# Layer 0 of a four-layer cross-attention kernel: each engine's order of stages written out by hand with other lags, and one MLP product moved from VectorE to GpSimd

## The reference

```
x1 = x  + SelfAttention(LN1(x))  Wao + bao      softmax(q k^T / 4 * mask - 10000 (1 - mask)) v
x2 = x1 + CrossAttention(LN2(x1), ctx) Wco + bco
y  = x2 + gelu(LN3(x2) W1 + b1) W2 + b2         W1: 256 x 1024, W2: 1024 x 256
gelu(h) = 0.5 h (1 + tanh(0.7978845608 h (1 + 0.044715 h^2)))
```

## Time and profile before

| | |
|---|---|
| median of 3 runs (lowest, highest) | 1527.47 us (1522.78, 1533.39) |
| the profiled execution | 1539.91 us |
| its span, first to last instruction | 1536.9 us |
| layer 0 in it, to the last write of `xs` (L765) | 0 to 647 us |
| layers 1 to 3 | 647 to 1537 us |
| busy over the span: PE, DVE, ACT, POOL | 1308.2, 943.9, 846.2, 491.9 us |
| mean granted PE clock | 0.927 |

### The profile page before, as it was taken

One profiled execution on the slowest core, in us unless ns is written; L12 is line 12 of the kernel. 1 busy time (PEld: TensorE's weight loads), 2 busy tenths in 40 slices (PEclk: granted clock), 3 DMA queues, 4 the chain that ended last, 5 costly groups with the idle time before them and its releaser, 6 DMA issues. The chain is left out here.

```text
span 1536.9 us, 31339 instructions
## 1 busy us (share of the span) xinstructions
PE 1308.2 (85%) x10866; PEld 1042.4 (68%) x10866; DVE 943.9 (61%) x1843; ACT 846.2 (55%) x2494; POOL 491.9 (32%) x490
## 2 busy tenths in 40 slices
PE   5777777777777775589999999999999999997797
PEld 3555566665666554478888887878878788885464
DVE  4566656565656544376667666676666666664354
ACT  4566565556565634365655555555555665653443
POOL 3343333333434321023333333333333333333000
PEclk8889898989888987889999999999999999998899
DMA  4030000000000000010000000000000000000110
GB/s 156 8 142 8 11 7 10 7 10 7 10 7 3 11 1 1 28 42 2 8 1 9 2 1 10 1 9 1 1 10 1 10 1 1 2 1 1 50 41 27
DMA packets 18578, 25.50 MB, mean 17 GB/s; under 512 B 1360, under 2 KB 16912, under 8 KB 18064
## 3 DMA queue, kind: packets, MB, share of 16 engines
q1 hardware_dynamic: 18448, 23.77, 4.7%
HBM read 21.67 MB, written 2.10 MB: 15 GB/s over the span
## 5 line engine op out<-in xcount | busy, mean ns | idle before, releaser
L1017 POOL TENSOR_TENSOR prob<-prob,l_z_inv 128x512 f32<-128x512 f32 x256 | 261.0, 1041 | 469.1 <-DVE l_z_inv L1258 469.1
L1177 ACT ACTIVATE prob<-psum,l_neg_max 128x256 f32<-128x256 f32 x512 | 236.0, 473 | 245.7 <-DVE l_neg_max L1252 245.7
L674 ACT ACTIVATE ring_e<-ring_e,neg_max 128x128 f32<-128x128 f32 x512 | 163.8, 394 | 142.9 <-DVE neg_max L795 142.9
L1252 DVE TENSOR_REDUCE l_neg_max<-psum 128x2 f32<-128x512 f32 x256 | 164.1, 683 | 14.9 <-PE psum L1071 14.9
L568 PE MATMUL psum<-ident,ring_e 128*128 128x128 f32 x512 | 89.7, 304 | 79.7 <-ACT ring_t L681 75.7
L1083 PEld LDWEIGHTS psum<-ident,prob 128*128 128x128 f32 x1024 | 110.8, 142 | 51.6 <-issue 48.0
L1099 PE MATMUL psum<-pT,vs 128*64 128x256 f32 x1024 | 139.9, 394 | 5.5 <-DVE aTl L1268 5.4
L1083 PE MATMUL psum<-ident,prob 128*128 128x128 f32 x1024 | 141.8, 281 | 1.3 <-issue 1.2
L568 PEld LDWEIGHTS psum<-ident,ring_e 128*128 128x128 f32 x512 | 68.3, 157 | 103.1 <-ACT ring_e L674 91.3
L450 POOL TENSOR_TENSOR ring_e<-ring_e,cross_add 128x512 f32<-128x512 f32 x64 | 81.5, 1287 | 169.7 <-DVE ring_e L790 169.7
L1263 DVE COPY pT<-psum 128x512 f32<-128x512 f32 x128 | 88.2, 689 | 57.1 <-PE psum L1083 57.0
(11 more groups left out here) (197 smaller groups left out, 3292.6 us busy)
## 6 DMA issues: line engine op xcount, KB each, us to landing
wz_raw<-wz_in SPq DMA_DIRECT2D x2, 1536.0 KB, 9.1
x_in<-x SPq DMA_DIRECT2D x8, 256.0 KB, 2.7
cT<-ctxT SPq DMA_DIRECT2D x8, 256.0 KB, 2.7
w<-w_in SPq DMA_DIRECT2D x2, 1024.0 KB, 11.5
l_ub<-ctx_in SPq DMA_DIRECT2D x8, 256.0 KB, 3.7
cg<-ctx_in SPq DMA_DIRECT2D x4, 512.0 KB, 3.8
out<-fin SPq DMA_DIRECT2D x4, 512.0 KB, 2.8
wi_raw<-wi_in SPq DMA_DIRECT2D x1, 1536.0 KB, 14.4
```

The source lines that it names most:

```text
L674: last = nc.scalar.activation(e, e, ACT.Exp, bias=neg_max[:, n % RE, h:h + 1])
L1017: pool.tensor_tensor(e, e, z_inv[:, t % RE, h, :].unsqueeze(2).broadcast_to([P, 2, D]), ALU.mult)\
L1177: last = nc.scalar.activation(prob[:, t % RE, h, qt * D:(qt + 1) * D], score_bank[h][:, qt * D:(qt + 1) * D], ACT.Exp, bias=neg_max[:, t % ...
L1252: nc.vector.tensor_reduce(neg_max[:, t % RE, h, :], score_bank[h].rearrange("p (t c) -> p t c", t=2), AX.X, ALU.max, negate=True).then_inc ...
```

## The change

All arithmetic of layer 0 stays, and layers 1 to 3 are untouched. Five things change.

1. **The order.** The loop over 16 steps is replaced on every engine by a written list of calls, `units(stage, s)` (this stage of unit s, counted from the body's first) and `pairs(stage, off)` (this stage of pair g + off). Blank lines part it into 16 slots. The table has them all; "mul" is `multiply`, "max" `maxima`, "exp" `exponentials`, "copy" `copy_turned`, "pv" is `sums` and `times_v`, "inv" is `invert` (the reciprocal, now a stage of its own), "arg" is the new `argument`, "st" `statistics`.

| slot | PE | ACT | DVE | POOL |
|---|---|---|---|---|
| 0 | cv, T0, turn -3 | tanh3, copy -4, exp -2 | mul 0, read cv, max -1, gated3 | add 0 |
| 1 | pv -8, turn -2, q | copy -3, read T0, exp -1 | mul 1, inv -8, max 0 | std2, add 1 |
| 2 | turn -1 | copy -2, exp 0 | mul 2, norm2, mul 3, divide -8, max 1 | add 2 |
| 3 | y0, scores 4, turn 0, T2 | copy -1, read q, exp 1 | max 2, out y0 | add 3 |
| 4 | k, turn 1 | copy 0, read T2, exp 2 | mul 4, max 3 | add 4 |
| 5 | pv -4, turn 2 | copy 1, exp 3, read k | mul 5, inv -4, max 4 | add 5 |
| 6 | y1, turn 3 | copy 2, exp 4 | mul 6, mul 7, divide -4, max 5 | add 6 |
| 7 | f0, scores 8, o, turn 4 | copy 3, exp 5 | out y1, max 6 | add 7 |
| 8 | f1, turn 5 | hidden0, copy 4, exp 6 | mul 8, max 7 | arg0, bias0, add 8 |
| 9 | pv 0, turn 6 | copy 5, hidden1, exp 7 | mul 9, poly0, read o and st1, inv 0, max 8 | add 9 |
| 10 | ck, f2, turn 7 | tanh0, copy 6, exp 8, read ck | mul 10, mul 11, poly1, divide 0, gated0, max 9, norm1 | std1, add 10 |
| 11 | f3, scores 12, turn 8 | hidden2, copy 7, tanh1, exp 9 | poly2, st0, max 10 | arg1, add 11 |
| 12 | T1, turn 9 | copy 8, hidden3, exp 10 | gated1, cross addend, mul 12, max 11 | bias2, std0, add 12 |
| 13 | pv 4, v, turn 10 | read T1, copy 9, exp 11 | mul 13, inv 4, max 12, read v | add 13 |
| 14 | cq, turn 11 | tanh2, copy 10, read cq, exp 12 | mul 14, mul 15, divide 4, poly3, max 13, gated2, norm0 | arg2, add 14, arg3 |
| 15 | co, scores 16, turn 12 | copy 11, exp 13 | read co and st2, max 14 | bias1, add 15 |

2. **The lags.** `exponentials` goes from s - 1 to s - 2, `turn` from s - 2 to s - 3, `copy_turned` from s - 2 to s - 4, the batch product from 6 steps to 9, `divide` from 7 to 10. Self units belong to pair g - 1 (before g), cross units to g - 3 (g - 2), the MLP's first product to g - 4 (g - 3), its second to g - 5 (g - 3). There are 13 bodies; 5 to 7 are the loop.
3. **The product with h** (L749 before, DVE) is `argument` on POOL.
4. **`times_v` is split**: `sums` comes first with a semaphore of its own.
5. **SP**: the three loads for layer 1 come before `next_x(1)`.

```diff
-        BODIES = R0 + 3
+        BODIES = R0 + 5
...
-        LIKE = 5
-        FILLED = [n for s in range(STEPS) for n in BESIDE.get(s, [])]
+        LIKE = 6
+
+        FILLED = [("cv", -3), ("T0", -1), ("q", -1), ("y0", -5), ("T2", -4), ("k", -1), ("y1", -5), ("f0", -4),
+                  ("o", -2), ("f1", -4), ("ck", -2), ("f2", -4), ("f3", -4), ("T1", -2), ("v", -1), ("cq", -2),
+                  ("co", -3)]
...
             a = int(s < U)
-            i = pair(j, g, -2 if a else 0)
+            i = pair(j, g, -3 if a else -1)
...
+            def units(stage, s):
+                if unit(j, g, s):
+                    stage(*unit(j, g, s))
+
+            def pairs(stage, off, *more):
+                if pair(j, g, off) is not None:
+                    stage(pair(j, g, off), g + off, *more)
...
-            next_x(1)
-            next_x(2)
-            next_ctx(1)
-
             for w, src, c in ((wz0_raw, "wz_in", 0), (wz1_raw, "wz_in", 1), (wi0_raw, "wi_in", 0)):
                 sp.dma_start(w[:, :], v[src][c * P:(c + 1) * P, :]).then_inc(l1_weights_in, 16)
...
+            for g in range(1, R0 + 2):
+                if g >= 3:
+                    next_ctx(g - 2)
+                    next_mask(g - 2)
+                if g < R0:
+                    next_x(g)
...
+            def argument(i, p, f):
+                t, h = ring_g[:, f % RH, :], ring_h[:, f % RH, :]
+                pool.wait_ge(*h_poly.at(i, f))
+                nc.gpsimd.tensor_tensor(t, t, h, ALU.mult).then_inc(h_arg.sem, 1)
...
+            def sums(a, i, u, ri, n):
+                pe.wait_ge(ones_made, 2)
+                pe.wait_ge(*probsT_done.at(ri, n + QUAD - 1))
+                pe.wait_ge(*heads_out.at(ri, n // QUAD - 1))
...
             def polynomial(i, f):
...
                 nc.vector.tensor_scalar(t, t, 0.044715, 1.0, ALU.mult, ALU.add).then_inc(h_poly.sem, 1)
-                dve.wait_ge(*h_poly.at(i, f))
-                nc.vector.tensor_tensor(t, t, h, ALU.mult).then_inc(h_arg.sem, 1)
...
+                pairs(linear, -4, "f3")
+                units(scores, 12)
+                units(turn, 8)
+
+                pairs(linear, -2, "T1")
+                units(turn, 9)
+
+                units(sums, 4)
+                units(times_v, 4)
+                pairs(linear, -1, "v")
+                units(turn, 10)
```

More of the change, by code:

```diff
@@ L297, in bodies @@
         def bodies(eng, body):
-            for g in range(3):
+            for g in range(5):
                 body(g, g)
-            with eng.Fori(3, R0) as j:
+            with eng.Fori(5, R0) as j:
                 body(j, LIKE)
@@ L452, in body @@
             def body(j, g):
[L453 to L472, removed]
+                units, pairs = stages(j, g)
+                units(add_mask, 0)
+                pairs(inverse_std, -4, 2)
+                units(add_mask, 1)
+                units(add_mask, 2)
+                units(add_mask, 3)
+                units(add_mask, 4)
+                units(add_mask, 5)
+                units(add_mask, 6)
+                units(add_mask, 7)
+                pairs(argument, -4, 0)
+                pairs(add_bias, -1, 0, x_ao, x_in, "bao", "o")
+                units(add_mask, 8)
+                units(add_mask, 9)
+                pairs(inverse_std, -2, 1)
+                units(add_mask, 10)
+                pairs(argument, -4, 1)
+                units(add_mask, 11)
+                pairs(add_bias, -4, 2, x_mlp, x_2, "b2", "y1")
+                pairs(inverse_std, 0, 0)
+                units(add_mask, 12)
+                units(add_mask, 13)
+                pairs(argument, -4, 2)
+                units(add_mask, 14)
+                pairs(argument, -4, 3)
+                pairs(add_bias, -2, 1, x_co, x_1, "bco", "co")
+                units(add_mask, 15)
             bodies(pool, body)
@@ L583, in times_v @@
                             at, h = (2 * j + t) * PAIR_ROWS, 2 * half + t
[L584 to L592, removed]
+                            last = nc.tensor.matmul(pv_bank[j * PAIR_ROWS:(j + 1) * PAIR_ROWS, half * P:(half + 1) * P],
+                                                    vm[a][:, b, half, at:at + PAIR_ROWS],
+                                                    ring_t[:, (n + j) % RE, h * P:(h + 1) * P], start=t == 0, stop=t == 1)
@@ L593, in times_v @@
                 last.then_inc(pv_done.sem, 1)
             def body(j, g):
[L596 to L617, removed]
@@ new lines, in body @@
+                units, pairs = stages(j, g)
+                pairs(linear, -3, "cv")
+                pairs(linear, -1, "T0")
+                units(turn, -3)
+                units(sums, -8)
+                units(times_v, -8)
+                units(turn, -2)
+                pairs(linear, -1, "q")
+                units(turn, -1)
+                pairs(linear, -5, "y0")
+                units(scores, 4)
+                units(turn, 0)
+                pairs(linear, -4, "T2")
+                pairs(linear, -1, "k")
@@ new lines, in body @@
+                units(turn, 1)
+                units(sums, -4)
+                units(times_v, -4)
+                units(turn, 2)
+                pairs(linear, -5, "y1")
+                units(turn, 3)
+                pairs(linear, -4, "f0")
+                units(scores, 8)
+                pairs(linear, -2, "o")
+                units(turn, 4)
+                pairs(linear, -4, "f1")
+                units(turn, 5)
+                units(sums, 0)
+                units(times_v, 0)
+                units(turn, 6)
@@ L619, in _ @@
+                pairs(linear, -3, "co")
+                units(scores, 16)
+                units(turn, 12)
             pe.wait_ge(consts_made, 1)
@@ new lines, in body @@
+                pairs(tanh, -5, 3)
+                units(copy_turned, -4)
+                units(exponentials, -2)
+                units(copy_turned, -3)
+                pairs(read, -1, "T0")
+                units(exponentials, -1)
+                units(copy_turned, -2)
+                units(exponentials, 0)
+                units(copy_turned, -1)
+                pairs(read, -1, "q")
+                units(exponentials, 1)
+                units(copy_turned, 0)
+                pairs(read, -4, "T2")
@@ new lines, in body @@
+                units(exponentials, 2)
+                units(copy_turned, 1)
+                units(exponentials, 3)
+                pairs(read, -1, "k")
+                units(copy_turned, 2)
+                units(exponentials, 4)
+                units(copy_turned, 3)
+                units(exponentials, 5)
+                pairs(hidden, -4, 0)
+                units(copy_turned, 4)
+                units(exponentials, 6)
+                units(copy_turned, 5)
+                pairs(hidden, -4, 1)
@@ new lines, in body @@
+                units(exponentials, 7)
+                pairs(tanh, -4, 0)
+                units(copy_turned, 6)
+                units(exponentials, 8)
+                pairs(read, -2, "ck")
+                pairs(hidden, -4, 2)
+                units(copy_turned, 7)
+                pairs(tanh, -4, 1)
+                units(exponentials, 9)
+                units(copy_turned, 8)
+                pairs(hidden, -4, 3)
+                units(exponentials, 10)
+                pairs(read, -2, "T1")
@@ L697, in _ @@
+                units(copy_turned, 9)
+                units(exponentials, 11)
+                pairs(tanh, -4, 2)
+                units(copy_turned, 10)
+                pairs(read, -2, "cq")
+                units(exponentials, 12)
+                units(copy_turned, 11)
+                units(exponentials, 13)
             act.wait_ge(w_cols, 16)
```

282 lines of the change are left out of this document (159 added, 123 removed).

## The result

The changed kernel takes **1399.07 us** (1396.74 to 1400.05), the kernel before, on the same chip, 1530.43: a ratio of 0.914 (0.909 to 0.919). The forecast was 1388, its range 1355 to 1460. The profiled execution took 1398.57 with a span of 1396.8, 140.1 less than before; as that execution of before lay 0.6% over its median, 131 of them are the change's.

What follows compares the result with a forecast made beforehand. The prediction held that the order of the queues, not a full engine, bounds layer 0. Its bodies summed to 508 us against 647, and the 139 us less, taken off the median 1527.47, gave 1388, range 1355 to 1460.

Steps and rivals of the forecast that it cites:

- The body: Full body of layer 0: the new order cuts it from 75.1 to 55 us, PE needing 48.1 at high clock.
- the walk: Slot-by-slot pass through the new order with durations from the trace: 51 us a full body, three PE waits remaining.
- The clock: PE in full bodies: runs at the high clock, since no remaining wait is as long as 2.89 us.
- The product on POOL: Product with h: takes 2.8 us a body from DVE, costs POOL 5.1 at 1.28 each, hidden.
- The collisions: DVE's normalise pairs beside POOL additions: up to 2.8 us a body, some already counted; bound below nothing.
- rival B: DVE held by whole POOL instructions: a body of about 62 us, total 1436; chance 0.22 including the ground up to the forecast.
- The start: First bodies of layer 0: x of pair 1 lands at about 36 us, 8 us lost once, bounds 0 and 11.
- The ends: Layer 0's filling and emptying bodies, summed one by one, tail 36 us; with full bodies layer 0 comes to 508.
- Layers 1 to 3: The later layers, 890 us, were taken as untouched, with no change in time.
- C: Full bodies take exactly 51 us and the ends are 12 us shorter: total 1360; chance 0.12.
- D: The chain across four engines stays the bound, PE's clock falls again: body 72 to 75, total 1505 to 1535; chance 0.08.
- E: Only fixed costs move (late x, end, longer lag), the body keeps 75.1 us: total 1546, slower; chance 0.06.

Runs made afterwards that it cites:

- e4: The changed kernel with four slots instead of two for the MLP's tiles (RH = 4): 1384.7 us, ratio 0.903.
- e9: The kernel before with 128 already met waits added on PE between layer 0 and layer 1: 1519.4 us in one execution.
- e1: The changed kernel with the product with h back on DVE, behind the polynomial: 1401.42 us, ratio 0.9155.
- e5: The changed kernel with DVE's constants() moved behind the first normalise of pair 0: 1397.58 us, ratio 0.910.
- e6: The changed kernel with constants() behind pair 0's first normalise and x of pair 1 issued ahead of the three 1536 KB loads: 1394.21 us, ratio 0.908.

## Why the prediction was right, and where its terms were off

**The body (55; measured 54.5).** The mechanism held: the order was the bound, and PE is now. The 48.1 us of PE's need were too few: at full clock e4 shows 50.3, and the 4 us added to the walk covered that. Three PE waits were named, 2.6 us. Two are there, 2.3 us, at turns 8 and 9 instead of 9 and 12, both behind ACT's `hidden` 2. The walk had it wait for nothing; it waits 2.19 us for a slot of `ring_h`, and with four slots both waits are gone. DVE's wait ahead of the reciprocal, 2 us in the walk, is 7.4 in the body.

**The clock.** I took the high level; 0.97 was measured in the full body, 1.00 in e4, against 0.86 of the earlier trace rows. The tail, where PE stands again, is at 0.83. The clock accounts for a third of the gain, the 7.0 of 20.6 us above; a body of before still took 72.6 us at 0.92 (e9).

**The product on POOL.** Priced 1.28 us, measured 1.27. The Trainium skill (GPSIMD Engine Reference, section 4.1) has GpSimd about twice as slow with two inputs, from which the prediction estimated 2.4 us a body lost. The factor agrees (1.27 against 0.69), and still e1 shows a gain of 1.9 us in the full body: POOL is busy for only 32.5 of 54.5 us. The tail is 4.4 us shorter in e1, where the sum had 2.4 for POOL's part.

**The collisions (within the 4 us allowed).** Lines of the full body, busy us, mean ns, idle before:

```profile
L885 DVE SCALAR_TENSOR_TENSOR hid<-ring_g,ring_h 128x512 f32<-128x512 f32 x5 | 5.3, 1060 | 0.0
...
L442 POOL TENSOR_TENSOR ring_g<-ring_g,ring_h 128x512 f32<-128x512 f32 x4 | 5.1, 1270 | 4.7 <-DVE ring_g L878 4.7
...
L846 DVE TENSOR_SCALAR ln<-x,mean_var,rstd 128x256 f32<-128x256 f32 x4 | 3.7, 971 | 0.0
```

`normalise` took a mean of 640 ns in the body before, now 971, `gated` 863, now 1060. With the product back on DVE (e1) they take 642 and 849 again, so the move is the cause. That is 4 x 0.33 + 5 x 0.20 = 2.3 us in this window, where the earlier trace rows gave up to 2.8. One of rival B's signs thus showed, longer `normalise` and `gated`, without its price: DVE comes to 44.7, not to 58.

**The start (8 us lost to x of pair 1; measured 3.1).** x landed near the 36 forecast: DVE went on at 34.6. The step that failed is the first multiply at 20.5, taken from the earlier trace rows: I missed that `constants()` now stands ahead of pair 0's `normalise`. Two delays lay one over the other. e5 takes away the first and the second grows to 9.38 us; e6 takes away both.

**The ends.** The term mis-sized is the sum's last: layer 0 ended at 519.4 instead of 508. By boundaries (forecast, its bodies cut at slot 12 by the lengths of the slots, and measured): start 72.5, 68.7; body 2 to 3 41, 47.4; 3 to 4 48.5, 50.9; four full ones 219, 217.0; the next 46, 46.7; from there to the last cross product's sum 45, 47.0; the tail 36, 41.9. The tail was taken as 33.8 plus POOL's part. But y0 of pair 6, which ran ahead of the last cross product's sum before (the first line below), now comes behind it, so that both second products of pairs 6 and 7 stand in the tail. The last wait for `gated` is 7.49 us instead of 4.24.

```profile
607.43 3.72 PE L510 MATMUL psum<-w,hid 128*128 128x256 f32 x16
```

```profile
480.00 5.41 PE L536 MATMUL psum<-w,hid 128*128 128x256 f32 x16 [2.54 <-DVE hid L885]
...
506.29 2.64 DVE L885 SCALAR_TENSOR_TENSOR hid<-ring_g,ring_h 128x512 f32<-128x512 f32 x2
508.98 9.93 PE L536 MATMUL psum<-w,hid 128*128 128x256 f32 x32 [7.49 <-DVE hid L885]
...
519.01 0.42 DVE L894 SCALAR_TENSOR_TENSOR xs<-psum,x_mlp 128x256 f32<-128x256 f32 x1 [3.04 <-PE psum L536]
```

16 matmuls take 5.41 us here, at a granted clock of 0.69, and 3.62 in the full body; the last 32 run at 0.72.

**Layers 1 to 3 (nothing; measured 12.9 less).** "Untouched" was true of their code and not of its place. This error and that of layer 0, 12 us each, cancel by luck: 508 and 890 make 1398, and the span was 1396.8.

**The base (11 us).** The forecast of 1388 is low for another reason. The 647 us of layer 0 were read from an execution of 1539.91 us, but the 139 us gained were taken off the median, 1527.47. Between the two lie 12 us. As far as the traces show they belong to the old layer 0, which ended at 637.3 to 649.1 with the same code, while layers 1 to 3 hardly vary. The 508 did not rest on them, so the gain from the median is smaller: the medians differ by 131 us.

**The rivals.** C (51 us a body) and B (62) missed on either side, D and E by 20 us a body. E's fixed costs were real, some 6.5 us at the start, of which 3.5 reach the end of layer 0 (e6), and 8 in the tail.

## What to carry to other kernels

Where no engine is full and in-order queues wait for each other in a ring, lags and places have to be changed together: here neither brought alone what it brought with the other. Once one engine is full, look for the ring buffer whose slot its feeder waits for; two more slots were worth 14 us here. The first and the last stretch of a pipeline get none of the gain (here 68.7 us against 62.3 as far as the first cross addend, and 41.9 against 33.8 in the tail), so they are summed stage by stage, with the clock that a standing PE has. And the times that a forecast takes from a profile are taken off that same execution, not off the median.

## What was not expected of the hardware

- The place of a PE loop's code changes its time: 877 to 907 us for the same instructions. The longer times come with stalls of up to 2.8 us at the turn of the loop that no other engine explains, and with 65 or 66 packets of instructions in these layers instead of 21. An experiment that adds instructions ahead of a loop should look at this before it blames anything else.
- In e5 a load of 256 KB, issued at 20.2 us behind 4.6 MB on the same queue, landed at about 34.5. In the change it was issued at 26.3 and landed at the same time.
